# Feed-forward products on pairs of 16-bit floats, block scales split on GpSimd, row sums on ScalarE

## The reference

```python
def fp4_quant_dequant(x):                 # blocks of 16 along the last dim
    xb = x.reshape(shape[:-1] + (shape[-1] // BLOCK, BLOCK))
    scale = jnp.maximum(jnp.max(jnp.abs(xb), axis=-1, keepdims=True) / 6.0, 1e-12)
    xn = xb / scale
    idx = jnp.searchsorted(_MID, jnp.abs(xn))
    return (_GRID[idx] * jnp.sign(xn) * scale).reshape(shape)
def fp4_linear(x, w):
    return jnp.einsum('bsk,nk->bsn', fp4_quant_dequant(x), fp4_quant_dequant(w))
def _L0_ffn_ref(x, w_gate, w_up, w_down):  # H = 256, I = 704
    gate, y = fp4_linear(x, w_gate), fp4_linear(x, w_up)
    return fp4_linear(jax.nn.silu(gate) * y, w_down)

x = x + 0.5 * ffn(_layernorm(x)); x = x + attn(_layernorm(x)); x = x + 0.5 * ffn(_layernorm(x))
```

## Time and profile before

| | |
|---|---|
| median of 3 runs | 3377.65 us (3376.19 to 3378.86) |
| the profiled execution | 3378.71 us, of which span 3376.6 us |
| busy in the span: TensorE | 3196.7 us (95%), 28848 matmuls |
| VectorE | 2747.1 us (81%) |
| ScalarE | 2365.3 us (70%) |
| GpSimd | 1500.9 us (44%) |
| mean granted TensorE clock | 0.987 |

### The profile page before, as it was taken

One profiled execution on the slowest core, in us unless ns is written; L12 is line 12 of the kernel. 1 busy time (PEld: TensorE's weight loads), 2 busy tenths in 40 slices (PEclk: granted clock), 3 DMA queues, 4 the chain that ended last, 5 costly groups with the idle time before them and its releaser, 6 DMA issues.

```text
span 3376.6 us, 77211 instructions
## 1 busy us (share of the span) xinstructions
PE 3196.7 (95%) x28848; PEld 2678.6 (79%) x28848; DVE 2747.1 (81%) x5326; ACT 2365.3 (70%) x4315; POOL 1500.9 (44%) x1666
## 2 busy tenths in 40 slices
PE   4999996999999999999999999999999998799998
PEld 4999995677777777777777777777777776799998
DVE  8999984877877887787787778878777777899996
ACT  3566652777777777778777777777777777465564
POOL 2243321544545545445445455455455453233331
PEclk9999998999999999999999999999999999899999
DMA  3133212222422332332233223224222333111110
GB/s 110 49 96 95 92 63 60 63 62 57 106 56 58 79 82 58 78 78 62 62 81 79 60 63 90 60 60 105 54 57 67 82 70 107 35 57 57 57 54 32
DMA packets 160353, 235.78 MB, mean 70 GB/s; under 512 B 30064, under 2 KB 71152, under 8 KB 159728
## 3 DMA queue, kind: packets, MB, share of 16 engines
q1 hardware_dynamic: 159984, 230.84, 26.0%
HBM read 95.49 MB, written 34.61 MB: 39 GB/s over the span
## 4 chain that ended last, share of the span: by engine, by line
PE 68%; issue 6%; DVE 5%; ACT 2%; POOL 2%; DVEq 0%; ACTq 0%; POOLq 0%
PE at_t_ps L1409 13%; PE at_o_ps L1425 10%; PE at_side_ps L1323 10%; PE ffn_gu_ps L505 7%; PE at_s_ps L1398 6%; PE at_s_ps L1399 6%; PE at_side_ps L1376 4%; PE ffn_down_ps L530 4%; PE at_side_ps L1335 4%; DVE at_e_rows L1591 2%; PE at_side_ps L1364 2%; ACT at_eT_hi L1507 1%; PE ffn_hT_ps L475 1%; DVE at_eT_lo L1597 1%; DVE at_v_masked L1569 1%
## 5 line engine op out<-in xcount | busy, mean ns | idle before, releaser
L1597 DVE SCALAR_TENSOR_TENSOR at_eT_lo<-at_t_ps,at_eT_hi 128x512 f16<-128x512 f32 (+3 forms) x1536 | 852.7, 555 | 471.5 <-ACT at_eT_hi L1507 445.2
L1499 ACT ACTIVATE at_e_rows<-at_e_rows,at_neg_max 128x1024 f32<-128x1024 f32 (+7 forms) x1024 | 792.2, 774 | 215.9 <-DVE at_neg_max L1591 214.5
L1507 ACT ACTIVATE at_eT_hi<-at_t_ps 128x512 f16<-128x512 f32 (+3 forms) x1536 | 745.1, 485 | 190.2 <-PE at_t_ps L1409 181.3
L1591 DVE CUSTOM_DVE_ANT_0 at_e_rows<-at_s_ps,at_strip,keep_s_scale 128x1024 f32<-128x1024 f32 (+7 forms) x1024 | 827.9, 809 | 10.2 <-PE at_s_ps L1399 7.5
L1409 PE MATMUL at_t_ps<-at_ident,at_e_rows 128*128 128x128 f32 x4608 | 801.0, 284 | 0.0
L1425 PE MATMUL at_o_ps<-at_v_cols,at_eT_hi 128*128 128x132 f16 x4608 | 610.6, 221 | 11.5 <-ACT at_o_raw L1518 7.1
L1425 PE MATMUL at_o_ps<-at_v_cols,at_eT_lo 128*128 128x66 f16 x4608 | 567.9, 193 | 0.0
L1398 PE MATMUL at_s_ps<-at_kh_st,at_q_st 128*128 128x512 f16 (+3 forms) x1536 | 501.8, 327 | 18.2 <-DVE at_acc L1581 12.5
L1425 PEld LDWEIGHTS at_o_ps<-at_v_cols,at_eT_hi 128*128 128x128 f16 x4608 | 432.9, 97 | 92.0 <-DVE at_eT_lo L1597 24.5
L1409 PEld LDWEIGHTS at_t_ps<-at_ident,at_e_rows 128*128 128x128 f32 x4608 | 492.9, 141 | 3.9 <-issue 0.5
L1399 PE MATMUL at_s_ps<-at_kl_st,at_q_st 128*128 128x512 f16 (+3 forms) x1536 | 481.6, 327 | 0.0
(11 more groups left out here) (226 smaller groups left out, 6957.7 us busy)
## 6 DMA issues: line engine op xcount, KB each, us to landing
at_kh_st<-at_k_hi SPq DMA_DIRECT2D x256, 128.0 KB, 2.3
at_kl_st<-at_k_lo SPq DMA_DIRECT2D x256, 128.0 KB, 2.4
at_w_qk<-w_qk_split SPq DMA_DIRECT2D x65, 256.0 KB, 3.0
at_q_st<-at_q_hi SPq DMA_DIRECT2D x128, 128.0 KB, 2.4
at_q_st<-at_q_lo SPq DMA_DIRECT2D x128, 128.0 KB, 2.4
at_w_v<-w_v_split SPq DMA_DIRECT2D x66, 128.0 KB, 2.4
ffn_x_rows<-in_L_attn_query_dram SPq DMA_DIRECT2D x32, 256.0 KB, 3.2
ffn_x_res<-in_L_attn_query_dram SPq DMA_DIRECT2D x32, 256.0 KB, 3.8
```

Source lines behind the costliest of these rows:

```text
L1499: nc.scalar.activation(e_rows[:, n % 4, :w], e_rows[:, n % 4, :w], ACT.Exp, bias=neg_max[:, n % 4:n % 4 + 1], scale=-1.0).then_inc(sem("ex ...
L1507: nc.scalar.activation(eT[0][:, i % EBUF, :count * P], t_ps[i % TBUF][:, :count * P], ACT.Copy, scale=PSCALE).then_inc(sem("eT_hi"), 1)
L1591: nc.vector.tensor_tensor_reduce(e_rows[:, n % 4, :w], s_ps[n % 2][:, col:col + w], strip[:, SEQ - w:], keep["s_scale"][:, 0:1], BIGGEST, ...
L1597: nc.vector.scalar_tensor_tensor(out=eT[1][:, i % EBUF, :count * P], in0=t_ps[i % TBUF][:, :count * P], scalar=PSCALE, in1=eT[0][:, i % EB ...
```

## The change

- The quantised values are no longer formed in 32 bits and split after turning. A value is code x scale with a code of few bits. Now the scale is split into two parts of 12 and fewer bits on GpSimd (`scales`: shift, subtract, subtract, subtract), and GpSimd multiplies the code with both parts in one instruction (`both_halves`) into two float16 halves. `h_q` and `x_q` hold both, twice the columns as before.
- TensorE turns the halves as 16-bit words (`transpose` with `ident_16`), into PSUM read as float16. `rest_inner` and `rest_rows` are gone; ScalarE copies out both halves in one instruction (1408 columns for the activations, 1024 for the rows). The last 64 rows of both halves share one tile of 128, so that there are 11 tiles, and the down product has 17 passes instead of 18.
- The weights are float16 halves too. So that they and the activations fit the range, powers of two are worked out from the largest value of each weight (`widen`, `spread_top`, `exponents`, `matched`, `fit`) and taken out again in silu, in `inner` and in the residual.
- Layer norm: ScalarE forms the sums (`row_sums`, a copy with an accumulated output) and the squares; `rstd` is no longer multiplied into the rows but into the scales of their blocks, on GpSimd. `row_stats` on VectorE is gone.
- `unit` and `coarse` are made in two halves each. `code` is bfloat16. `scale` and `parts` exist once, so that `block_max` waits for `parts` of the set before.
- The raw weights and their scales get buffers of their own, and the first pass's buffers start 15 KB higher.

```diff
-        scale = sb("scale", [P, 2, NB])
...
+        code = sb("code", [P, WIDE], BF16)
+        h_q = sb("h_q", [P, 2, 2, 2 * IPAD], F16)
+        x_q = sb("x_q", [P, 2, W2], F16)
...
+        xT = sb("xT", [P, 2, 2, KT, W2 // KT], F16)
...
-        xT_ps = ctx.enter_context(nc.psum_tensor(f"{tag}_xT_ps", [P, 512], F32))
+        xT_ps = ctx.enter_context(nc.psum_tensor(f"{tag}_xT_ps", [P, 1024], F16))
         hT_ps = ctx.enter_context(nc.psum_tensor(f"{tag}_hT_ps", [P, 1024], F32))
+        hT_ps16 = hT_ps[:].bitcast(F16)
...
+        def set_halves(i):
+
+            a, b = set_cols(i)
+            middle = a + (b - a) // (2 * QB) * QB
+            return (a, middle), (middle, b)
...
-            def row_stats(m, k, turn):
...
-                    nc.vector.bn_stats(stats[:, j, :], x[:, j * HID:(j + 1) * HID]).then_inc(sem("stats"), 1)
...
-                nc.vector.tensor_tensor(xT[1][:, par].rearrange("p k n -> p (k n)"), xT_ps[:],
...
-                nc.vector.tensor_tensor(halves(raw[:, j * INNER:(j + 1) * INNER]), halves(silu[:, j, :]), up_cols, ALU.mult).then_inc(sem("h"), 1)
+                nc.vector.scalar_tensor_tensor(out=halves(raw[:, j * INNER:(j + 1) * INNER]), in0=up_cols, scalar=keep["ffn"][:, 1:2],
+                                               in1=halves(silu[:, j, :]), op0=ALU.mult, op1=ALU.mult).then_inc(sem("h"), 1)
...
+                if has_set(i - 1):
+                    dve.wait_ge(sem("parts"), i + AHEAD_X)
                 nc.vector.tensor_reduce(amax[:, blk], blocks_of(raw[:, a:b]), AX.X, ALU.max, apply_absolute_value=True).then_inc(sem("amax"), 1)
...
-                nc.vector.tensor_scalar(scale[:, par, blk], amax[:, blk], SIXTH, MIN_SCALE, ALU.mult, ALU.max).then_inc(sem("scale"), 1)
...
-                nc.vector.tensor_tensor(blocks_of(unit[:, a:b]), blocks_of(raw[:, a:b]), per_block(recip[:, blk], (b - a) // QB),
-                                        ALU.mult).then_inc(sem("unit"), 1)
+                for a, b in set_halves(i):
+                    nc.vector.tensor_tensor(blocks_of(unit[:, a:b]), blocks_of(raw[:, a:b]), per_block(recip[:, a // QB:b // QB], (b - a) // QB),
+                                            ALU.mult).then_inc(sem("unit"), 1)
...
-                nc.vector.scalar_tensor_tensor(out=x_out[:, k, :], in0=down_ps[:], scalar=0.5, in1=x_res[:, k, :],
+                nc.vector.scalar_tensor_tensor(out=x_out[:, k, :], in0=down_ps[:], scalar=keep["ffn"][:, 4:5], in1=x_res[:, k, :],
...
+            def centre(m, par):
+
+                pool.wait_ge(sem("sums"), 2 * m + 2)
+                nc.gpsimd.tensor_scalar(mean[:, par], sums[:, par], -1.0 / HID, None, ALU.mult).then_inc(sem("mean"), 1)
...
             def root(m, par):
 
+                pool.wait_ge(sem("squares"), 2 * m + 2)
+                nc.gpsimd.tensor_scalar(var_eps[:], squares[:, par], LN_EPS, None, ALU.add).then_inc(sem("var_eps"), 1)
...
-                nc.gpsimd.tensor_tensor(mean[:, par], zero[:], moments[:, par, :, 0], ALU.subtract).then_inc(sem("mean"), 1)
...
-                nc.gpsimd.tensor_tensor(rstd[:, par], var_eps[:, par], power[:], ALU.pow).then_inc(sem("rstd"), 1)
...
+                nc.gpsimd.tensor_tensor(rstd[:], var_eps[:], power[:], ALU.pow).then_inc(sem("rstd"), 1)
...
+            def scales(i):
+
+                a, b = set_cols(i)
+                blk, n = slice(a // QB, b // QB), i + AHEAD_X + 1
+                pool.wait_ge(sem("tied"), n)
+                if has(i):
+                    nc.gpsimd.tensor_scalar(scale[:, :2 * HB], amax[:, :2 * HB], keep["ffn"][:, 2:3], keep["ffn"][:, 3:4],
+                                            ALU.mult, ALU.max).then_inc(sem("h_scale"), 1)
+                if has(i + AHEAD_X):
+                    m = i + AHEAD_X
+                    nc.gpsimd.tensor_scalar(scale[:, 2 * HB:], amax[:, 2 * HB:], SIXTH * FSCALE, MIN_SCALE * FSCALE, ALU.mult, ALU.max).then_inc(sem("x_scale"), 1)
+                    pool.wait_ge(sem("x_scale"), m + 1)
+                    pool.wait_ge(sem("rstd"), m + 1)
+                    x_scale = scale[:, 2 * HB:].rearrange("p (j b) -> p j b", b=XB)
+                    nc.gpsimd.tensor_tensor(x_scale, x_scale, rstd[:].unsqueeze(2).broadcast_to([P, 2, XB]), ALU.mult).then_inc(sem("x_fit"), 1)
+                    pool.wait_ge(sem("x_fit"), m + 1)
+                if has(i):
+                    pool.wait_ge(sem("h_scale"), i + 1)
+                nc.gpsimd.tensor_scalar(shifted[:, blk], scale[:, blk], HALVES, None, ALU.mult).then_inc(sem("shifted"), 1)
+                pool.wait_ge(sem("shifted"), n)
+                nc.gpsimd.tensor_tensor(rest[:, blk], shifted[:, blk], scale[:, blk], ALU.subtract).then_inc(sem("rest"), 1)
+                pool.wait_ge(sem("rest"), n)
+                nc.gpsimd.tensor_tensor(parts[:, 0, blk], shifted[:, blk], rest[:, blk], ALU.subtract).then_inc(sem("high"), 1)
+                pool.wait_ge(sem("high"), n)
+                nc.gpsimd.tensor_tensor(parts[:, 1, blk], scale[:, blk], parts[:, 0, blk], ALU.subtract).then_inc(sem("parts"), 1)
+
+            def both_halves(out, cols, blk):
+
+                n = blk.stop - blk.start
+                return nc.gpsimd.tensor_tensor(out, blocks_of(code[:, cols]).unsqueeze(1).broadcast_to([P, 2, n, QB]),
+                                               parts[:, :, blk].unsqueeze(3).broadcast_to([P, 2, n, QB]), ALU.mult)
...
+            def scale_rows(m):
...
+                both_halves(x_q[:].rearrange("p s (b e) -> p s b e", e=QB), slice(XCOL, WIDE), slice(2 * HB, NB)).then_inc(sem("x_q"), 1)
...
+                pool.wait_ge(sem("parts"), m + AHEAD_X + 1)
...
-                                        per_block(scale[:, par, j * HB:(j + 1) * HB], HB), ALU.mult).then_inc(sem("h_q"), 1)
...
+                both_halves(edge, slice(j * INNER + last, (j + 1) * INNER), slice(j * HB + last // QB, (j + 1) * HB)).then_inc(sem("h_edge"), 1)
+                both_halves(whole, slice(j * INNER, j * INNER + last), slice(j * HB, j * HB + last // QB)).then_inc(sem("h_q"), 1)
...
-                    root(i + 4, k % 2)
+                    centre(i + 4, k % 2)
+                if has(i + 3):
+                    root(i + 3, (k + 1) % 2)
+                if has_set(i):
+                    scales(i)
...
-                a, b = set_cols(i)
-                act.wait_ge(sem("unit"), i + AHEAD_X + 1)
-                nc.scalar.activation(coarse[:, a:b], unit[:, a:b], ACT.Abs, scale=2.0 ** 22).then_inc(sem("coarse"), 1)
+                for n, (a, b) in enumerate(set_halves(i)):
+                    act.wait_ge(sem("unit"), 2 * (i + AHEAD_X) + (n + 1))
+                    nc.scalar.activation(coarse[:, a:b], unit[:, a:b], ACT.Abs, scale=2.0 ** 22).then_inc(sem("coarse"), 1)
...
-                nc.scalar.activation(xT[0][:, par].rearrange("p k n -> p (k n)"), xT_ps[:], ACT.Copy).then_inc(sem("xT_hi"), 1)
...
+                nc.scalar.activation(xT[:, par].rearrange("p s k n -> p (s k n)"), xT_ps[:], ACT.Copy).then_inc(sem("xT"), 1)
...
-                nc.scalar.activation(hT[part][:, j].rearrange("p k n -> p (k n)"), hT_ps[:, :IPAD], ACT.Copy).then_inc(sem(("hT_hi", "hT_lo")[part]), 1)
+                nc.scalar.activation(hT[:, j].rearrange("p k n -> p (k n)"), hT_ps16[:, :2 * INNER], ACT.Copy).then_inc(sem("hT"), 1)
...
+            def row_sums(m, k, turn):
+                act.wait_ge(sem(f"x_loaded{k}"), turn * 16 + 16)
+                for j in range(2):
+                    nc.scalar.activation(junk[:, 0, k % 2, j], x_rows[:, k, j * HID:(j + 1) * HID], ACT.Copy, accum_out=sums[:, k % 2, j:j + 1]).then_inc(sem("sums"), 1)
...
             def row_norm(m, k):
-                act.wait_ge(sem("rstd"), m + 1)
+                act.wait_ge(sem("mean"), m + 1)
...
-                    act.wait_ge(sem("unit"), m)
+                    act.wait_ge(sem("unit"), 2 * m)
...
                 for j in range(2):
-                    nc.scalar.activation(raw[:, XCOL + j * HID:XCOL + (j + 1) * HID], x_rows[:, k, j * HID:(j + 1) * HID], ACT.Identity,
-                                         bias=mean[:, k % 2, j:j + 1]).then_inc(sem("centred"), 1)
-                act.wait_ge(sem("centred"), 2 * m + 2)
+                    nc.scalar.activation(rows_of[j], x_rows[:, k, j * HID:(j + 1) * HID], ACT.Identity, bias=mean[:, k % 2, j:j + 1]).then_inc(sem("xn"), 1)
...
                 for j in range(2):
...
+                    nc.scalar.activation(junk[:, 1, k % 2, j], rows_of[j], ACT.Square, scale=HID ** -0.5, accum_out=squares[:, k % 2, j:j + 1]).then_inc(sem("squares"), 1)
...
-                nc.scalar.activation(halves(silu[:, j, :]), gate_cols, ACT.Silu).then_inc(sem("silu"), 1)
+                nc.scalar.activation(halves(silu[:, j, :]), gate_cols, ACT.Silu, scale=keep["ffn"][:, 0:1]).then_inc(sem("silu"), 1)
...
-                    out_inner(i - 2, 0, 0)
-                if has(i - 2):
-                    out_inner(i - 2, 0, 1)
```

(54 more changed lines are left out.)

193 lines of the change are left out of this document (97 added, 96 removed).

## The result

The changed kernel took 3583.5 us (median, 3582.5 to 3584.1) against 3377.5 for the kernel before on the same chips: 1.061 of its time, 95% interval 1.059 to 1.063. Its profiled execution has a span of 3582.2 us, 205.6 more than before.

What follows compares the result with a forecast made beforehand. TensorE bounds the kernel now; after the change GpSimd, 11.9 us plus 6.2 shut out less 0.5, 17.6 a step. Steps +173, splits +18, start +8, fill +3, last steps -6 on 3378.7: 3574 us, range 3430 to 3640.

Steps and rivals of the forecast that it cites:

- Rival 2: VectorE's `unit`, `total` and `code` let GpSimd's 16-bit products through; TensorE sets 12.6 to 13.0 a step, 3299 us; chance 0.12.
- Rival 3: 16-bit products and turns don't shorten TensorE, 14.7 us a step; about 3400 us without exclusion; chance 0.04.
- Rival 1: Same exclusion, but long holds fall beside VectorE's PSUM work, maximum and reciprocal; step 15 to 16, 3420 to 3475 us; chance 0.16.
- The step: Steady feed-forward step: GpSimd's 11.9 us plus 6.2 shut out, minus about 0.5, makes 17.6 (14.8 to 18.4) against 14.39.
- Products: GpSimd's products of h and x for both halves, per step: 7.5 to 8.2 us, taken as 7.9.
- Scalar operations: Three scalar operations on GpSimd per step, taken at 0.37 us each, 1.1 in all.
- Waits and starts: GpSimd per step: seven waits for itself of 0.08, 0.55 us, less 0.2 for starts that overlap.
- Shut-out time: VectorE's `tied`, `unit`, `total` and `code` hold the port 6.2 us a step, minus about 0.5 for starts done meanwhile.
- 54 steps: Steps of both feed-forward passes in which everything runs, 27 each, going from 14.39 to 17.6 us: +173.
- The splits of the attention weights: In 16 steps of the first pass, 1.15 us each with GpSimd the bound: +18, bounds 0 and 19.
- Start of the first pass: Weight exponents add a reduction, copy, turn and small operations per weight, GpSimd seven linked small ones: +8, bounds 3 and 12.
- Last three steps: Last three steps of each pass, with no x part, go to about 13 us: -6, bounds -10 and 0.

Runs made afterwards that it cites:

- Experiment 1: The changed kernel with a one-input block maximum of `total` in place of `code` from the second set of each pass: 3471.9 us, ratio 1.028 to the kernel before.
- experiment 2: The changed kernel without the two middle operations of the scale split on GpSimd (`shifted`, `rest`): 3520.9 us, ratio 1.043 to the kernel before.
- experiment 3: The kernel before with an unused spare product of 1248 elements on GpSimd in each step, behind the power: 3445.3 us, ratio 1.020.
- experiment 6: The changed kernel with h and x written once in 32 bits, halves split after the turn, block scales on VectorE: 3339.2 us, ratio 0.989 to the kernel before.

## Why the prediction was right, point by point

**The mechanism.** The prediction said that GpSimd and VectorE shut each other out for whole instructions and that GpSimd would never idle. Experiment 1 shows the exclusion by taking it away from one instruction, experiment 2 that GpSimd's own work counts in full, experiment 3 that `unit`, for which no row stood, is among the colliding ones. Rival 2 (no exclusion) falls with experiments 1 and 3. Rival 3 (16-bit products not shorter) falls with experiment 6. Rival 1 (the ports pack well) falls with the changed kernel's own timeline: no operation of GpSimd is hidden under `total`, `code` or `unit`, only stretched by them.

One reading of mine was wrong without harm. I wrote that all of GpSimd's 4.7 us in the kernel before fall beside operations that don't collide. Its power (3117.84 to 3118.54 in the earlier trace rows) runs beside `tied`, a scalar operation of the colliding kind, and `tied` keeps its length on VectorE's timeline of the kernel before:

```profile
3117.98 0.22 DVE L293 TENSOR_SCALAR ffn_tied<-ffn_amax 128x120 f32<-128x120 f32 x1
```

So not every GpSimd instruction shuts VectorE out to its end: the products do, this power of two columns doesn't. In my sum the power stands with its own length only, so nothing hung on it.

**The step:** 17.6 forecast, 18.01 measured, within the bounds of 14.8 and 18.4. Term by term, from the timeline above:
- Products: 7.9 forecast, 7.39 measured (twice 2.73 and 1.93). They cost the 1.7 ns an element of the 32-bit ones, (1.93 - 0.19) / 1024, and not the 1.90 of the earlier trace rows; I had gone between the two. That row, which I had read as a product on 16-bit operands, is a subtraction that reads one 32-bit and one 16-bit tensor.
- Scalar operations: 1.1 forecast, 1.51 measured (0.67, 0.32, 0.52). The dearest is the one whose factors come from a buffer (88 columns, 0.67).
- The other small ones came as forecast: two-operand steps 1.32 for 1.2, the power 0.72, mean and variance 0.4 when not held.
- Waits and starts: 0.35 net forecast (0.55 less 0.2), 0.66 measured, the step of 18.01 less the 17.35 that the operations last. With it GpSimd's own part is 12.24 for 11.9.
- Shut-out time: 6.2 less 0.5 forecast, 5.77 measured: 1.93 at the mean, 2.02 at the variance, 1.82 at the second pair of h products.

My order of the turns was off: I had `tied` wait for the rows' product and the first half of `unit` for the second large h product. `tied` waited for the first large h product, the first half of `unit` for the rows' product, and the two h products of the second pair then waited for one half of `unit` each. The sum does not depend on who goes first, as long as GpSimd never idles, and that is why it held. The wait of the block maximum for `parts`, 1.5 growing to 3.4, is 3.04 in the steady part.

**The sum:** +196 forecast, +205.6 measured, both against the profiled execution. By the starts of the block maxima:
- 54 steps: +173 forecast. From set 2 to 29 the second pass lost 97.1 us in 27 steps, 3.6 each, so 54 are +194: 21 more than forecast.
- The splits of the attention weights: +18 forecast. A step with one is 18.96 (e.g. 189.70 to 208.66), 0.94 more, so 16 are +15.
- Not forecast: two steps of the first pass of the kernel before were themselves 2.7 and 1.2 us longer than 14.39, which the changed kernel does not show, and its own first full step there was 1.4 shorter than the later ones: -5.3 together.
- Start of the first pass: +8 forecast, 3.4 up to set 2 and 0.3 ahead of it. Fill of the second: +3 forecast, -1.7.
- Last three steps: -6 forecast, -1.6 in each pass, -3.2. Attention and the end: 0 forecast, +2.8.

So the forecast's nearness, 9.6 us in 206, is partly luck: the step was 0.4 us too short, which is 21 us, and start, fill, splits and the slow steps of before gave 17 of them back, against 6 the other way. The term that was mis-sized is GpSimd's own part, by its small operations and its waits.

**The other signs.** TensorE was forecast at some 75% busy and is at 77.5; GpSimd near 95% and is at 95.3; the clock below 1.00 and is at 0.95. The low clock costs nothing here. Two steps of the changed kernel, one at full clock and one not, in the columns of the earlier trace rows:

```profile
3091.85:3109.87 18.02, 13.23 (x115) 9.39 (x112) 14.61 (x11) 9.58 (x17) 17.23 (x15) 1.00 0.13 45
3308.04:3326.05 18.01, 14.91 (x111) 9.87 (x110) 14.60 (x11) 9.57 (x17) 17.22 (x16) 0.88 0.15 45
```

TensorE is busy 1.7 us longer in the second, and the step is as long. In the first its matmuls cost, from start to start, 0.150 us (352 columns), 0.109 (256) and 0.056 (turns), which for 48, 34 and 30 of them makes the 12.6 us forecast.

## What to carry to other kernels

Before work is given to GpSimd, add to its own time the whole length of every VectorE instruction that collides with it: here GpSimd's 12.2 us fitted into a step of 14.4, and with VectorE's 5.8 they made 18.0. Where it must be used, place it beside VectorE's PSUM operands, reductions and row statistics, and look for a tiny scalar operation in that window, since one of 0.17 us was held to the end of the product. The sum is for a GpSimd that never idles; where it has time to spare, what counts is which VectorE instruction it holds. And change the operands' format and the way they are made in separate steps: here the first, with the new layer norm, was a gain of 38 us and the second a loss six times as large.

## What the runs showed of the hardware that I had not expected

- A reduction of 1920 columns from SBUF and the row statistics run beside GpSimd without either getting longer (2.15 us; 0.75 for two), while a scalar operation on two columns waits to the end of GpSimd's instruction (1.32 us for 0.17).
- GpSimd's power on two columns (0.70 us) does not hold VectorE: `tied` keeps its 0.22 us beside it in the steady steps of the kernel before.
- Products on GpSimd from bfloat16 and float32 to float16 cost what float32 ones cost, 1.7 ns an element.
- On GpSimd a one-tensor operation with constants is dearer than a two-tensor one of the same 120 columns (0.52 against 0.44), and 0.67 for 88 columns with factors from a buffer.
- An operation of GpSimd held up for a long time costs nothing where GpSimd has time to spare, and hardly touches the VectorE instruction that holds it: 1.03 us for 0.24, beside `unit` 2.27 for 2.23.
- A TensorE busy for 99.8 of 100 us was not the bound of its step: the step lost another 0.14 us without a change to its work.
